# A two-layer graph network: key and query products from halves, and y moments in the first layer

## The reference

```
h = relu(layernorm(x));  y = x + layer0(h, adj)      # 8 Euler steps of a graph diffusion
h = relu(layernorm(y));  out = y + layer1(h, adj, adj)
layer1(x, L, adjacency):
    h  = relu(layernorm((2 L / lam_max - I) @ x @ Wc + bc) * g1 + be1)
    x1 = h + x
    q, k, v = x1 @ Wq, x1 @ Wk, x1 @ Wv              # 4 heads of 32 features
    attn = softmax(where(adjacency > 0, q k^T / sqrt(32), -1e9))
    x2 = layernorm(x1 + (attn @ v) @ Wo + bo) * g2 + be2
    return layernorm(x2 + gelu(x2 @ W1 + b1) @ W2 + b2) * g3 + be3
```

## Time and profile before

| | us |
|---|---|
| three runs | 867.37, 867.99, 868.82 (median 867.99) |
| the profiled execution | 868.01 |
| its span, first to last instruction | 866.2 |

### The profile page before, as it was taken

One profiled execution on the slowest core, in us unless ns is written; L12 is line 12 of the kernel. 1 busy time (PEld: TensorE's weight loads), 2 busy tenths in 40 slices (PEclk: granted clock), 3 DMA queues, 4 the chain that ended last, 5 costly groups with the idle time before them and its releaser, 6 DMA issues.

```text
span 866.2 us, 18914 instructions
## 1 busy us (share of the span) xinstructions
PE 818.8 (95%) x6609; PEld 690.4 (80%) x6609; DVE 646.5 (75%) x2146; ACT 530.5 (61%) x1223; POOL 310.4 (36%) x406
## 2 busy tenths in 40 slices
PE   6999999999999999998999999999999999999992
PEld 5778989898989888976777777777777777778982
DVE  5956464645477656536899999999999998987998
ACT  4434243434322422325988888898888888887884
POOL 2011121212122415300445545555554545432654
PEclk9999999999999999998999999999999999999997
DMA  6000010101010100312434455423344444322243
GB/s 133 1 13 13 13 37 13 37 14 37 13 37 13 37 25 26 101 46 76 119 94 108 133 136 135 134 94 96 96 124 135 135 136 133 103 49 63 82 139 97
DMA packets 57514, 65.59 MB, mean 76 GB/s; under 512 B 5574, under 2 KB 32844, under 8 KB 57420
## 3 DMA queue, kind: packets, MB, share of 16 engines
q1 hardware_dynamic: 57120, 64.25, 26.6%
q10 hardware_dynamic: 300, 0.13, 0.1%
HBM read 39.59 MB, written 24.77 MB: 74 GB/s over the span
## 4 chain that ended last, share of the span: by engine, by line
PE 21%; DVE 12%; issue 8%; POOL 8%; ACT 3%; DMA 1%; DVEq 0%; SPq 0%; POOLq 0%
PE bank L1896 6%; PE bank L1954 4%; PE bank L1916 4%; PE bank L1882 3%; DVE prob L2062 2%; PE bank L381 2%; POOL z_norm L353 2%; POOL z_gain L349 2%; POOL x_bo L1834 2%; DVE stats L1666 2%; ACT prob L2004 2%; POOL rstd_b L230 2%; PE bank L385 1%; DVE prob L1661 1%; DVE z L2101 1%
## 5 line engine op out<-in xcount | busy, mean ns | idle before, releaser
L2004 ACT ACTIVATE prob<-prob,low 128x512 f32<-128x512 f32 x256 | 183.7, 718 | 28.2 <-DVE low L2062 25.8
L2062 DVE CUSTOM_DVE_ANT_0 prob<-bank,mask 128x512 f32<-128x512 f32 x256 | 171.0, 682 | 8.5 <-PE bank L1882 6.3
L1896 PE MATMUL bank<-ident,prob 128*128 128x128 f32 x1024 | 158.3, 277 | 1.4 <-ACT probT L1987 1.0
L1896 PEld LDWEIGHTS bank<-ident,prob 128*128 128x128 f32 x1024 | 120.8, 141 | 42.1 <-issue 30.6
L1882 PE MATMUL bank<-k_stack,q_stack 96*128 96x512 f32 x256 | 124.1, 485 | 8.6 <-DVE low L2062 7.3
L1987 ACT ACTIVATE probT<-bank 128x512 f32<-128x512 f32 x176 | 103.1, 586 | 22.9 <-PE bank L1896 21.4
L880 PE MATMUL bank<-B_hi,halves 128*128 128x384 f32 x384 | 106.7, 341 | 3.0 <-DVE C L1276 1.6
L851 PE MATMUL bank<-halves,P3T_hi 128*128 128x256 f32 x512 | 93.9, 285 | 0.9 <-DVE halves L1292 0.5
L851 PEld LDWEIGHTS bank<-halves,P3T_hi 128*128 128x128 f32 x512 | 80.5, 191 | 4.4 <-DVE halves L1292 1.3
L880 PEld LDWEIGHTS bank<-B_hi,halves 128*128 128x128 f32 x384 | 70.6, 189 | 6.4 <-DVE halves L1263 2.7
L851 PE MATMUL bank<-halves,P3T_lo 128*128 128x256 f32 x256 | 72.4, 283 | 0.0
(11 more groups left out here) (277 smaller groups left out, 1919.4 us busy)
## 6 DMA issues: line engine op xcount, KB each, us to landing
k_stack<-bounce_q SPq DMA_DIRECT2D x48, 256.0 KB, 4.0
q_stack<-bounce_k SPq DMA_DIRECT2D x48, 256.0 KB, 5.5
bounce_q<-k_parts SPq DMA_DIRECT2D x32, 256.0 KB, 2.2
bounce_k<-q_parts SPq DMA_DIRECT2D x32, 256.0 KB, 3.8
x_in<-in_x_dram SPq DMA_DIRECT2D x16, 256.0 KB, 2.8
spread<-inverse_sums SPq DMA_DIRECT2D x64, 64.0 KB, 2.1
out_dram<-probT SPq DMA_DIRECT2D x16, 256.0 KB, 2.4
y_shifted<-y_staging SPq DMA_DIRECT2D x14, 256.0 KB, 2.1
```

The lines of the kernel that those rows point to most:

```text
L1896: last = pe.transpose(psum[2 + u % 2][:, mt * P:(mt + 1) * P], prob[u % RING][:, mt * P:(mt + 1) * P], ident[:, :])
L2004: act.activation(prob[u % RING][:, :], prob[u % RING][:, :], ACT.Exp, bias=low[:, u % TURNED:u % TURNED + 1], scale=-1.0, accum_out=row_su ...
L2062: dve.tensor_tensor_reduce(prob[u % RING][:, :], psum[u % 2][:, :], mask[:, u // HEADS, :], 1.0, 3e38, ALU.add, ALU.min, low[:, u % TURNED ...
```

## The change

Key and query product of batches 1 to 15 are each three fp32r products of halves. Wk and Wq are split once, at the start of the second layer, by GpSimd. x1 turned is split in every round: its high half by ScalarE at u = 2, its low half by VectorE at u = 3 (both in the buffer of the query's halves), and its f32 copy, which the value product still needs, by ScalarE at u = 3, after the low half. Keys and queries move: key product from u = 3 to 4 (the query's stays at 4), high halves to 4 and 5, low halves to 5 and 6. The convolution uses bank B and waits for the spread sums' row instead of the query's low half; `conv_weights` now waits for that. The y moments and the `h_scales` of batches 0 to 12 are all made in the first layer, as `MOMENTS_AT` says, into tiles that hold all batches; rounds 11 to 13 still make those of 13 to 15.

```diff
+MOMENTS_AT = {2: (0, 1), 3: (2, 3), 4: (4, 5), LAM_PAIR: (6, 7), KEY_PAIR: (8,), PAIRS: (9, 10, 11, 12)}
-AT_X1, AT_X1T, AT_X1T_OUT, AT_K, AT_Q, AT_K_HI, AT_Q_HI, AT_K_LO, AT_Q_LO = 1, 2, 2, 3, 4, 3, 4, 4, 5
+AT_X1, AT_X1T, AT_X1T_HI, AT_X1T_LO, AT_X1T_OUT = 1, 2, 2, 3, 3
+AT_K, AT_Q, AT_K_HI, AT_Q_HI, AT_K_LO, AT_Q_LO = 4, 4, 4, 5, 5, 6
# first layer, GpSimd, pair(p)
-                    if p == LAM_PAIR - 1:
-                        for b in range(2):
-                            h_scales(pool, one, b, b)
 ...
+                    for done in MOMENTS_AT.get(p, ()):
+                        h_scales(pool, one, done)
 ...
-                h_scales(pool, one, 2, 0)
+                for b in MOMENTS_AT[PAIRS]:
+                    h_scales(pool, one, b)
# first layer, VectorE, pair(p)
                     early(p, "T_lo2")
+                    for done in MOMENTS_AT.get(p, ()):
+                        y_moments(dve, one, done)
                     early(p, "q")
# second layer, GpSimd
-                    if within(r, 0, BATCH - 3):
-                        h_scales(pool, one, r + 2, s)
+                    if within(r, MOMENTS_AT[PAIRS][-1] - 1, BATCH - 3):
+                        h_scales(pool, one, r + 2)
+                pool.wait_ge(one.weights_loaded, 16 * 5)
+                for n, (source, (hi, lo)) in enumerate(((one.Wks, Wk_parts), (one.Wqs, Wq_parts))):
+                    pool.tensor_copy(hi[:, :], source[:, :]).then_inc(W_split, 1)
+                    pool.wait_ge(W_split, 2 * n + 1)
+                    pool.tensor_tensor(out=lo[:, :], in0=source[:, :], in1=hi[:, :].bitcast(F32),
+                                       op=ALU.subtract).then_inc(W_split, 1)
# second layer, TensorE
+                def split_product(pe, bank, parts):
+                    for n, (w, x) in enumerate(products(parts, x1T_parts)):
+                        last = pe.matmul(bank[:, :], w[:, :], x, start=n == 0, stop=n == 2)
+                    return last
                         if u == AT_K and enters:
                             at_least(pe, oT_ready, r - 2)
-                            k_product(pe, one, psum[7 - s], r)
+                            pe.wait_ge(W_split, 4)
+                            pe.wait_ge(x1T_split, 2 * r)
+                            split_product(pe, psum[7 - s], Wk_parts).then_inc(one.k_psum, 1)
                         if u == AT_Q and enters:
-                            q_product(pe, one, A_BANK, r)
+                            pe.wait_ge(x1T_ready, r + 1)
+                            split_product(pe, A_BANK, Wq_parts).then_inc(one.q_psum, 1)
                             if u == AT_CONV:
-                                pe.wait_ge(q_lo_ready, r + 1)
+                                pe.wait_ge(sums_row_ready, r - 1)
 ...
-                                last = pe.matmul(A_BANK[:, :], h_part[:, k, :], L_part[:, k, :],
+                                last = pe.matmul(B_BANK[:, :], h_part[:, k, :], L_part[:, k, :],
                         if u == AT_Z and within(r, 0, BATCH - 2):
+                            pe.wait_ge(q_lo_ready, r + 1)
                             conv_weights(pe, one, A_BANK, r + 1)
# second layer, ScalarE
+                        if u == AT_X1T_HI and enters:
+                            act.wait_ge(one.x1T_psum, r + 1)
+                            act.wait_ge(one.q_hi_written, 16 * r)
+                            act.activation(x1T_parts[0], A_BANK[:, :], ACT.Copy).then_inc(x1T_split, 1)
                         if u == AT_X1T_OUT and enters:
+                            act.wait_ge(x1T_split, 2 * r)
                             x1T_out(act, one, A_BANK, r)
# second layer, VectorE
-                        if u == AT_Y_MOMENTS and within(r, 0, BATCH - 3):
+                        if u == AT_Y_MOMENTS and within(r, MOMENTS_AT[PAIRS][-1] - 1, BATCH - 3):
                             y_moments(dve, one, r + 2)
+                        if u == AT_X1T_LO and enters:
+                            dve.wait_ge(x1T_split, 2 * r - 1)
+                            dve.wait_ge(one.q_lo_written, 16 * r)
+                            dve.tensor_tensor(out=x1T_parts[1], in0=A_BANK[:, :],
+                                              in1=x1T_parts[0].bitcast(F32), op=ALU.subtract
+                                              ).then_inc(x1T_split, 1)
```

More of the change, by code:

```diff
@@ L159, in two_layers @@
         one.stats = tensor(whole, "stats_a", [P, NT, 6])
-        one.mv = tensor(whole, "mv_a", [P, NT, 2])
+        one.mv = tensor(whole, "mv_a", [P, BATCH, NT, 2])
         one.var_eps = tensor(whole, "ve_a", [P, NT])
-        one.rstd = [tensor(whole, f"rstd_a{i}", [P, NT]) for i in range(2)]
+        rstd_a, shift_a = (tensor(whole, n, [P, BATCH, NT]) for n in ("rstd_a", "shift_a"))
+        one.rstd, one.shift = ([tile[:, b, :] for b in range(BATCH)] for tile in (rstd_a, shift_a))
         one.minus_one = tensor(whole, "minus_one", [P, NT])
         one.mean_rstd = tensor(whole, "mean_rstd_a", [P, NT])
-        one.shift = [tensor(whole, f"shift_a{i}", [P, NT]) for i in range(2)]
         one.h = [tensor(whole, f"h{i}", [P, NT, D]) for i in range(2)]
@@ L230, in inverse_root, with h_scales @@
     pool.tensor_tensor(out=rstd[:, :], in0=var_eps[:, :], in1=exponent[:, :], op=ALU.pow).then_inc(pool_step, 1)
-def h_scales(pool, one, b, s):
-    inverse_root(pool, b, one.mv, one.mv_ready, one.var_eps, one.rstd[s], one.pool_step, one.h_ready, NT * (b - 1),
+def h_scales(pool, one, b):
+    inverse_root(pool, b, one.mv[:, b, :, :], one.mv_ready, one.var_eps, one.rstd[b], one.pool_step, one.scales, 2 * b,
                  one.exponent, one.pool_waited)
     pool.wait_ge(one.pool_step, 2 * b + 2)
-    pool.tensor_tensor(out=one.mean_rstd[:, :], in0=one.mv[:, :, 0], in1=one.rstd[s][:, :],
+    pool.tensor_tensor(out=one.mean_rstd[:, :], in0=one.mv[:, b, :, 0], in1=one.rstd[b],
                        op=ALU.mult).then_inc(one.scales, 1)
     pool.wait_ge(one.scales, 2 * b + 1)
-    pool.tensor_tensor(out=one.shift[s][:, :], in0=one.mean_rstd[:, :], in1=one.minus_one[:, :],
+    pool.tensor_tensor(out=one.shift[b], in0=one.mean_rstd[:, :], in1=one.minus_one[:, :],
                        op=ALU.mult).then_inc(one.scales, 1)
@@ L250, in normalise @@
     act.activation(one.h[s][:, t, :], one.y[:, bass.ds(b * N + t * D, D)], ACT.Relu,
-                   scale=one.rstd[s][:, t:t + 1], bias=one.shift[s][:, t:t + 1]).then_inc(one.h_ready, 1)
+                   scale=one.rstd[b][:, t:t + 1], bias=one.shift[b][:, t:t + 1]).then_inc(one.h_ready, 1)
 def all_tiles(one, row):
@@ L315, in y_moments @@
 def y_moments(dve, one, b):
-    moments(dve, b, lambda t: one.y[:, bass.ds(b * N + t * D, D)], one.stats, one.stats_ready, one.mv, one.mv_ready,
-            one.scales, 2 * b, one.dve_waited)
+    moments(dve, b, lambda t: one.y[:, bass.ds(b * N + t * D, D)], one.stats, one.stats_ready,
+            one.mv[:, b, :, :], one.mv_ready, one.scales, 0, one.dve_waited)
 def z_moments(dve, one, b):
@@ L570, in layer0 @@
         x0_hi_ready, x0_lo_ready = sem("x0_hi_ready"), sem("x0_lo_ready")
-        PT_hi_ready, PT_lo_ready, B_hi_ready, B_lo_ready = (
-            sem(n) for n in ("PT_hi_ready", "PT_lo_ready", "B_hi_ready", "B_lo_ready"))
+        PT_hi_ready, PT_lo_ready, B_split = (
+            sem(n) for n in ("PT_hi_ready", "PT_lo_ready", "B_split"))
         C_psum = sem("C_psum")
@@ L1384, in early @@
                         q_lo_out(dve, one, SQ_BANK, 0)
-                    if step == (1, "y2"):
-                        y_moments(dve, one, 2)
                 def trace_out(p, place):
@@ L1723, in layer1 @@
         z2_std = sb("z2_std", [P, NT, D])
+        x1T_parts = tuple(one.q_parts[:, part, :] for part in range(2))
+        Wk_parts, Wq_parts = (tuple(sb(f"{n}_{part}", [P, D], F32R) for part in ("hi", "lo")) for n in ("W_k", "W_q"))
+        x1T_split, W_split = sem("x1T_split"), sem("W_split")
         one.x1[1], one.v[1] = sb("x1_1", [P, NT, D]), sb("v_1", [P, NT, D])
@@ L1761, in layer1 @@
         rstd3 = [row_sums[0][:, i * NT:(i + 1) * NT] for i in range(RING)]
-        shift3 = [*one.rstd, *one.shift]
+        shift3 = one.shift[0:RING]
         y_be3_ready, stats3_ready, mv3_ready, pool3, scales3, z3_std_ready, z3_gain_ready, result_ready = (
@@ L2026, in round_ @@
                         if u == AT_CONV_OUT and within(r, 0, BATCH - 2):
-                            conv_out(act, one, A_BANK if r > 1 else psum[7], r + 1)
+                            conv_out(act, one, B_BANK if r > 1 else psum[7], r + 1)
                         if (r, u) == AT_W1_HI:
```

20 lines of the change are left out of this document (6 added, 14 removed).

## The result

The changed kernel takes **880.5 us** (median of 4 runs, 879.9 to 882.5) against 867.7 (4 runs, 867.4 to 868.8): a ratio of 1.0150, with a 95% interval of 1.0135 to 1.0164. The forecast was 878.8, with a range of 869 to 883.5. The profiled execution took 880.5 as well, with a span of 878.7 (before: 868.0 and 866.2).

The account below looks back on a forecast made before the run. Three engines nearly full, with TensorE and VectorE tied at scores 8, were taken to bound the kernel; 7.8 + 0.75 + 0.15 + 2.4 - 0.3 = +10.8 us on 868.0 gave 878.8 us, range 869 to 883.5.

Parts of the forecast that it names:

- the tie at scores 8: Second layer, each round: scores product 8 may not start before mask 6, so VectorE work before it costs like TensorE work.
- The walk through units 3 to 8: Round at 500, row by row: VectorE's low half and a 0.8 us idle gap make scores 8 start +0.6 us later.
- (b): Rival: the low half is hidden and only TensorE's own path moves, 13 x 0.13 us; 872.7 us, chance 0.13.
- TensorE's saving: Key and query products as three fp32r products each: 0.23 + 0.16, about 0.39 us of TensorE a round, in 15 rounds.
- The weights' splits: GpSimd's four splits of the weights are needed only at unit 4 of round 1: priced at 0.
- Rounds 1, 2 and 3 to 15: Second layer: round 1 +0.75 us (ScalarE's copy and waiting), round 2 +0.15, rounds 3 to 15 13 x 0.6 = 7.8.
- Pair 5: First layer: this pair loses its two y moments, where TensorE had waited 1.25 us for GpSimd's sum: -0.3, bounds 0 and -1.6.
- The end of the layer: First layer's drain pair: GpSimd's work for four moments runs to 397.95 and ends the block later, +2.4 us, bounds 0 and 4.
- The port: First residual on VectorE against GpSimd's cast of h, both wanting one port: sum unchanged, bounds -1.4 and +4.6 us.
- (a): Rival: TensorE is the bound and VectorE's lateness is swallowed, 15 x -0.39 us, layer's end +2.1: 864.2 us, chance 0.13.
- (c): Rival: the residual loses the port in every round from the new phase, +4.6 us: 883.4 us, chance 0.09.
- (d): Rival: the change doesn't do all it says, moments 13 to 15 stay in the second layer; priced at 0.

## Why the prediction was right

- **The bound, and the tie at scores 8.** Right. TensorE at 95% was not the whole bound: 0.60 us more for VectorE ahead of mask 6 moved scores 8 by 0.61, and doubling the low half cost the same again. The 0.6 is no price of the low half as such: with the key's halves one unit earlier the low half stood where it did, and a round cost 0.1.
- **The walk through units 3 to 8.** Right in its order and its sums: mask 6 9.71 us after the reciprocal (the walk: 9.11 + 0.60), idle time ahead of the key's low half 0.75 (walk: 0.8). Undoing that idle time alone gave 6.0 of the 12.8 back. Wrong in the walk: it says that TensorE does not stand still ahead of the key product. Done with scores 5, TensorE stands there 0.66 us (0.21 before); that costs nothing while mask 6 decides, and became the next bound when that was mended. And the 0.13 us by which TensorE alone would come late does not follow from the walk, which ends the query product at 502.6 against 502.59. The trace has 0.12 (6.37 against 6.25 after the reciprocal), so that number was luck; rival (b) uses it, the forecast does not.
- **TensorE's saving.** Too high by a fifth. I had the convolution's three products, 0.70, for both; the key's take 506.74 - 505.96 = 0.78 and the query's 0.68, so 0.33 is saved and not 0.39.
- **y moments in the rounds: 0.** Right, shown from both sides: without them rounds stay at 24.75, with them back at 25.33.
- **Convolution, bounce buffers: 0.** No wait of any size on them shows in the trace. No run took them out one by one.
- **The weights' splits: 0.** Nobody waits for the splits themselves, but they are not free. They hold GpSimd from 398.35 to 399.88 at the start of the second layer, so its first x1_bo starts 1.68 us after the first scores and not 0.13 after them, and meets round 1's first residual, which takes 1.65 us instead of 0.69 (rows below, under the port). TensorE waits for it:

```profile
401.96 1.12 PE L370 MATMUL bank<-ident,x 128*128 128x128 f32 x4 [0.78 <-DVE x L363]
```

It starts to turn x1 3.59 us after the first scores, against 2.62 before. This first residual is long (1.36 to 1.66 us) in all nine profiles with the split products and 0.69 in all five without. How much of the 0.97 reaches the end of round 1 no run shows.
- **Rounds 1, 2 and 3 to 15.** +0.74 and +0.18 against +0.75 and +0.15. That of round 1 is luck in its size: the sum behind it lacks the long residual, and the way to round 2 takes 27.10 to 28.8 us in the profiles with the split products (29.4 with the low half doubled) and 26.0 to 27.6 in those without. Rounds 3 to 15 +8.1 against 7.8. Round 15 took 1.03 of that, not 0.6; with the key's halves early it took 0.2, so most of it is of the same cause.
- **Round 16.** Not in the sum, and +1.07 in the profiles. It is the clock and not a wait, and perhaps chance; its place is below.
- **Pair 5.** TensorE's idle 1.25 us became 0.34. TensorE's last work of the layer ended 0.8 us earlier than before (394.09 against 394.87); over the six profiles with this first layer the difference runs from -1.5 to +0.05 with a mean of -0.5, so -0.3 is within what profiles differ by, and not shown. The products alone, with the moments of three batches in the first layer, are at 393.18 there, and only one profile has the order of before.
- **The end of the layer.** Right, partly by luck: GpSimd began at 389.55, 0.8 earlier than I had, and each batch took 2.19 and not 1.90, since 0.28 us of latency lies between two; it ended at 398.01, forecast 397.95. +2.45 net, +2.1 forecast. The kernels with two and with four batches' scales in the last pair show the cause.
- **The port.** Two long residuals instead of three, -0.46, well inside the bounds; the kernels here had from 0 to 3 of them. In the other rounds it is the cast that is long: at 476.72 both start, the residual takes 0.69 and the cast 1.16. Round 1 shows a longer case, VectorE's residual beside GpSimd's x1_bo:

```profile
400.25 1.65 DVE L363 SCALAR_TENSOR_TENSOR x<-z_norm,h 128x512 f32<-128x512 f32 x1
```

```profile
400.05 1.31 POOL L1831 TENSOR_TENSOR x_bo<-x,bc_all 128x512 f32<-128x512 f32 x1
```

GpSimd's ends at 401.36, and the residual ends 0.54 later, at 401.90, as if it had begun its work (0.6 to 0.7 us) only then. By the rule of the Trainium skill ("SBUF — State Buffer", section "SBUF: two separate sides"), that the two exclude each other for a whole instruction, it should be so; the trace agrees.
- **Rivals.** (a) fell: the VectorE work isn't swallowed. (b), that only TensorE's own path moves, fell with mask 6 at 9.71 and the wait for it; the kernel with the key's halves early is what (b) describes, at +0.1 a round. (c) did not come. (d) is what the text of the kernel says, at 0.

The sum was 10.8 and the change is 12.5 in the profiles: 1.07 of the missing 1.7 is round 16, 0.35 the layer change (2.45 against 2.1), 0.3 the rounds 3 to 15. The last stands at 0.3 only because one first residual fewer was long (-0.4).

## What to carry to other kernels

When several engines are each some 90% busy, price an added instruction by its place: find the next instruction on which two engines tie, and count what stands ahead of it, idle gaps included. An order that fits one set of durations leaves a gap with another; here moving two lines by one unit was worth 6.0 us, more than the faster products could ever give (0.33 a round, 5 us in all). Work moved to an "idle" engine at the end of a stage is paid if that engine is the last one to finish, and an instruction moved later takes with it everything queued behind the waits for it.

## What the runs showed of the hardware

**Half clock for longer or shorter, or not at all.** After the change of layers the granted clock falls to half for some microseconds in 13 of the 14 profiles, and how many differs: 3.4 to 13.7 us (of the stretch from 380 to 460), 6.8 both in the kernel of before and in the changed one. Stretches of 3 us, TensorE's busy time, its clock; the kernel with the moments alone, the changed kernel, and the kernel of before with the moments of batches 0 to 10, in which it does not fall:

```profile
405.00:408.00 3.00, 2.88 (x7) 0.50 0.00 0
```

```profile
405.00:408.00 3.00, 1.34 (x5) 0.89 0.00 0
```

```profile
405.00:408.00 3.00, 2.34 (x13) 1.00 0.79 267
```

It does not follow the length of TensorE's gap: among the kernels with a gap of 1.05 or 1.06 us it lasted 0, 3.4, 6.8 (the kernel of before) and 10.2 us, and in the changed kernel, with a gap of 4.28, 6.8. Without the split products the way to round 2 took 25.98 us with none of it, 26.46 with 3.4, 26.03 and 26.36 with 6.8, and 27.64 with 13.7: the longest goes with 1.3 to 1.7 us more. With the split products the two go together less well (27.10 to 27.83 us at 6.8, 27.72 to 28.77 at 10.2).

**Round 16.** TensorE waits 1.23 us there for a mask, in the kernel of before (first row) as in the changed one. In the changed one what follows runs at half clock:

```profile
772.84 0.49 PE L1882 MATMUL bank<-k_stack,q_stack 96*128 96x512 f32 x1 [1.23 <-DVE low L2062]
```

```profile
784.29 0.58 PE L1885 MATMUL bank<-k_stack,q_stack 96*128 96x512 f32 x1 [1.23 <-DVE low L2079]
784.80 1.94 PE L1924 MATMUL bank<-probT,v 128*32 128x128 f32 x32
```

(1.94 us instead of the 1.08 of other rounds, and of before at this place.) The same wait stands in eleven profiles: in eight of them the clock fell behind it, for 3.4 us, and round 16 took 22.0 to 22.1 us; in three, of before among them, it stayed, and the round took 20.9. In the three kernels with the statistics late also in the last rounds the wait is gone, the clock stayed, and the round took 20.3. So the wait alone does not decide. The eight are of kernels with and without the products, one of them (the moments of batches 0 to 10) no slower than before, and each kernel has one profile: whether it is chance or phase stays open.
